# A first conditioning computed by halves, its second half behind the first projections of an attention layer

## The reference

```python
def _bi_wkv(r, k, v, w, u, time_emb):          # r = x, k = v = f
    tf = sigmoid(sum(time_emb, axis=-1))
    decay = exp(-exp(w)) * (0.5 + 0.5 * tf)
    ek = exp(minimum(k, 30.0)); ekv = ek * v
    # nf, df: a = a * decay + ekv_t, b = b * decay + ek_t, forward in time; nb, db backward
    euk = exp(minimum(u + k, 30.0))
    num = nf + nb - ekv + euk * v
    den = df + db - ek + euk
    return sigmoid(r) * (num / maximum(den, 1e-08)) * (0.8 + 0.2 * tf)
x = x + attention(_bi_wkv(x, f, f, L0_cond_w, L0_cond_u, cond))     # 32 query heads, 8 key heads, rope, causal softmax
x = x + ffn(_bi_wkv(x, f, f, L0_cond2_w, L0_cond2_u, cond))         # and so on, three more layers
```

## Time and profile before

| | us |
|---|---|
| median of 3 runs (lowest, highest) | 1380.36 (1378.04, 1382.36) |
| the profiled execution | 1380.08 |
| its span in the trace | 1378.3 |
| start and pieces of conditioning 0, until VectorE's last quotient | 0 to 62.3 |
| first matmul | 65.31 |
| first row maxima (group 0) | 82.90 |
| normalization of groups 0, 16, 32, 48, 63 starts at | 89.76, 159.67, 235.68, 311.67, 380.23 |
| end of the attention stage, next stage's sigmoid | 393.20 |

### The profile page before, as it was taken

One profiled execution on the slowest core, in us unless ns is written; L12 is line 12 of the kernel. 1 busy time (PEld: TensorE's weight loads), 2 busy tenths in 40 slices (PEclk: granted clock), 3 DMA queues, 4 the chain that ended last, 5 costly groups with the idle time before them and its releaser, 6 DMA issues. The chain is left out here.

```text
span 1378.3 us, 16687 instructions
## 1 busy us (share of the span) xinstructions
PE 1143.8 (83%) x5770; PEld 824.8 (60%) x5770; DVE 976.2 (71%) x1977; ACT 611.9 (44%) x1423; POOL 535.9 (39%) x440
## 2 busy tenths in 40 slices
PE   0179899999979888999599957999999966189997
PEld 0045556555557765333388846888888842068876
DVE  7868988888758996944533536888888868954354
ACT  2156666666655545345154424333333326033333
POOL 4437767676503221530064323444444410405520
PEclk9999999999989999999699978999999988579999
DMA  2032122121011102200543421111010000011101
GB/s 93 12 88 56 38 50 62 39 63 26 21 33 46 39 24 82 102 0 1 204 153 135 174 73 56 32 32 32 32 31 31 5 8 31 0 48 46 46 28 61
DMA packets 31091, 73.41 MB, mean 53 GB/s; under 512 B 5362, under 2 KB 15091, under 8 KB 28192
## 3 DMA queue, kind: packets, MB, share of 16 engines
q1 hardware_dynamic: 28432, 67.44, 15.8%
q0 software_dynamic: 1536, 3.86, 0.9%
q10 hardware_dynamic: 1040, 1.05, 0.2%
HBM read 55.89 MB, written 6.29 MB: 45 GB/s over the span
## 5 line engine op out<-in xcount | busy, mean ns | idle before, releaser
L175 POOL TENSOR_TENSOR sums<-scans 128x512 f32<-128x512 f32 x64 | 88.2, 1378 | 314.1 <-ACT terms L169 173.0
L531 ACT ACTIVATE probs<-ps_s,stats 128x256 f32<-128x256 f32 (+1 forms) x256 | 104.3, 419 | 58.9 <-DVE stats L621 57.5
L722 PE MATMUL ps_p<-xin,wkvq 128*128 128x512 f32 x148 | 74.0, 624 | 67.6 <-DVE xin L238 65.3
L195 DVE RECIPROCAL sums<-sums 128x256 f32<-128x256 f32 x64 | 112.1, 1752 | 2.0
L478 POOL TENSOR_TENSOR probs<-probs,stats 128x512 f32<-128x512 f32 x64 | 67.4, 1053 | 118.6 <-DVE stats L627 118.6
L621 DVE CUSTOM_DVE_ANT_0 ps_s<-ps_s,mask 128x256 f32<-128x256 f32 (+1 forms) x256 | 82.9, 383 | 8.9 <-PE ps_s L746 8.7
L180 POOL TENSOR_TENSOR sums<-sums,terms 128x512 f32<-128x512 f32 x64 | 85.5, 1336 | 5.0
L722 PEld LDWEIGHTS ps_p<-xin,wkvq 128*128 128x128 f32 x148 | 26.5, 199 | 88.5 <-issue 84.8
L920 POOL TENSOR_TENSOR L3hid<-L3hid,L3sig 128x1024 f32<-128x1024 f32 x17 | 46.1, 2719 | 75.4 <-DVE L3hid L1046 37.8
L1888 PE MATMUL K_ps_kvp<-K_wqkv_hi,K_xin_hi 128*128 128x256 f32 x256 | 75.4, 294 | 0.0
L1793 ACT ACTIVATE K_ks<-K_ps_kvp 128x256 f32<-128x256 f32 x64 | 24.6, 385 | 110.9 <-PE K_ps_kvp L1888 110.9
(11 more groups left out here) (393 smaller groups left out, 3449.9 us busy)
## 6 DMA issues: line engine op xcount, KB each, us to landing
E_fc<-l_fc_dram SPq DMA_DIRECT2D x16, 1024.0 KB, 7.2
qswap<-qraw SPq DMA_DIRECT2D x60, 128.0 KB, 2.3
K_wqkv<-l_wqkv_dram SPq DMA_DIRECT2D x16, 384.0 KB, 3.2
L3wgu<-L_w_dram SPq DMA_DIRECT2D x17, 256.0 KB, 2.6
L0wgu<-L_w_dram SPq DMA_DIRECT2D x14, 256.0 KB, 2.6
L3wdn<-L_w_dram SPq DMA_DIRECT2D x17, 128.0 KB, 2.1
wkvq<-w_l0a_dram SPq DMA_DIRECT2D x4, 512.0 KB, 4.2
wo<-w_l0a_dram SPq DMA_DIRECT2D x4, 512.0 KB, 3.7
```

Of the source, the lines that this page charges most:

```text
L175: pstep.mark(pool.tensor_tensor(sums[:, k, :, :], scans[:, k, :, 0, :], scans[:, k, :, 1, :], ALU.add))
L195: dstep.mark(dve.reciprocal(den, den))
L531: ins = act.activation(dst[:, i % 2, :], src[:, i % 2, :], ACT.Exp, bias=stats[:, g % 4, 4 + i:5 + i], scale=-1.0, accum_out=stats[:, g % ...
L722: ins = pe.matmul(ps[:, :], w[:, k, :], xin[:, k, h * HALF:(h + 1) * HALF], start=(k == 0), stop=(k == CH - 1))
```

## The change

Conditioning 0 is computed in the order `HALF_FIRST`, so that the first four pieces give the first half of the columns. Five pieces (with four quotients) and the product of the first half stay in `stage_first`; the barrier comes then, and the three other pieces, the last four quotients and the second half's product follow inside the attention stage. `START` projects the first half first: k0, q00, v0, q10. Its last two items run behind the scores of groups 0 and 1. The pieces of conditioning 1 go 1, 2, 2, 3 over the pairs. In `stage_first` the loads are reordered (`crep`, `vecs`, then `fside` by halves), and bound, exponential and inner product also go by halves, the second inner product behind the scans of the second piece. Shifts of the rotation in pair 0: the second half's `rope_first` in group 1 rather than 0, `rope_cos`, `rope_sin`, `rope_add` of q1 one group later.

```diff
+HALF_FIRST = (0, 1, 4, 5, 2, 3, 6, 7)
...
-                sp.dma_start(fside[:, :, :], io["fT"]).then_inc(s_f, 16)
+                sp.dma_start(crep[:, :, :], io["cond"]).then_inc(s_c, 16)
                 sp.dma_start(vecs[:, :], io["vecs"]).then_inc(s_vec, 16)
-                sp.dma_start(crep[:, :, :], io["cond"]).then_inc(s_c, 16)
+                for h in range(2):
+                    sp.dma_start(fside[:, :, halves[h]], io["fT"][:, :, halves[h]]).then_inc(s_f[h], 16)
...
+                for p in range(FIRST_PIECES):
+                    if p == FIRST_PIECES - 1:
+                        act.wait_ge(s_x, 16)
+                        condition_act(act, sig_first)
+                    piece_act(act, 0, HALF_FIRST[p], p % 2)
...
-                block_dve(dve, 0)
+                for p in range(FIRST_PIECES):
+                    if p == FIRST_PIECES - 1:
+                        dve.wait_ge(s_ekv, 2)
+                    piece_scans(dve, 0, HALF_FIRST[p], p % 2)
+                    if p == 1:
+                        bound_inner(1)
+                    if p:
+                        piece_finish(dve, 0, HALF_FIRST[p - 1], (p - 1) % 2)
+                dstep.wait()
+                condition_half(dve, 0, sig_first, 0)
...
-            START = ("k0", "q00", "k1", "q01", "v0", "v1", "q10", "q11")
+            START = ("k0", "q00", "v0", "q10", "k1", "q01", "v1", "q11")
+            AHEAD = 6
...
-                condition_act(act, sig)
-                for what in START:
-                    evac(0, what)
+                for p in range(FIRST_PIECES, NP):
+                    piece_act(act, l, HALF_FIRST[p], p % 2)
+                    for what in START[2 * (p - FIRST_PIECES):2 * (p - FIRST_PIECES) + 2]:
+                        evac(0, what)
...
+                        if g < len(START) - AHEAD:
+                            evac(0, START[AHEAD + g])
...
-                condition_dve(dve, l, sig)
+                for p in range(FIRST_PIECES, NP):
+                    piece_scans(dve, l, HALF_FIRST[p], p % 2)
+                    piece_finish(dve, l, HALF_FIRST[p - 1], (p - 1) % 2)
+                dve.wait_ge(s["ld_rope"], 32)
+                rope_first(0, "k", 0)
+                rope_first(0, 0, 0)
+                piece_finish(dve, l, HALF_FIRST[NP - 1], (NP - 1) % 2)
+                dstep.wait()
+                condition_half(dve, l, sig, 1)
+                for h, what, step in ((0, "k", 1), (0, "k", 2), (0, 0, 1), (0, 0, 2)):
+                    rope_first(h, what, step)
...
-                        if g == 0:
+                        if g == 1:
...
-                        if u in (0, 3):
+                        if u in (0, 3) and c:
                             for step in (0, 1, 2) if u == 0 else (3, 4):
-                                piece_scan(dve, l + 1, 2 * c, 0, step)
...
+                        if c == LAST and u in (12, 13):
+                            for step in (0, 1, 2) if u == 12 else (3, 4):
+                                piece_scan(dve, *next_piece(NP - 1), step)
                 pt_evac(ALL - 3)
                 recip(ALL - 1)
                 pt_evac(ALL - 2)
                 pt_evac(ALL - 1)
+                piece_finish(dve, *next_piece(NP - 1))
...
-                for what in START:
+                for what in START[:AHEAD]:
                     item(0, what)
                 for c in range(L0_PAIRS):
                     for u in range(NU):
                         g = c * NU + u
                         score(g)
+                        if g < len(START) - AHEAD:
+                            item(0, START[AHEAD + g])
```

More of the change, by code:

```diff
@@ L144, in turn_of @@
     def turn_of(l, i):
+        if l < 2:
+            return NP * l + HALF_FIRST.index(i)
         group = next(g for g in TOGETHER if l in g)
@@ L229, in condition_act, with condition_half @@
             act.activation(sig[:, :, half], xT[:, :, half], ACT.Sigmoid).then_inc(sig_ready, 1)
[L231 to L236, removed]
+    def condition_half(dve, l, sig, h):
+        dve.wait_ge(sig_ready, 2 * l + h + 1)
+        for b in (2 * h, 2 * h + 1):
             c = slice(b * T, (b + 1) * T)
@@ L262, in stage_first @@
             block = st.enter_context(nc.Block())
+            halves = (slice(0, HALF), slice(HALF, NT))
             @block.sync
             def _(sp):
-                sp.dma_start(fside[:, :, :], io["fT"]).then_inc(s_f, 16)
+                sp.dma_start(crep[:, :, :], io["cond"]).then_inc(s_c, 16)
                 sp.dma_start(vecs[:, :], io["vecs"]).then_inc(s_vec, 16)
-                sp.dma_start(crep[:, :, :], io["cond"]).then_inc(s_c, 16)
+                for h in range(2):
+                    sp.dma_start(fside[:, :, halves[h]], io["fT"][:, :, halves[h]]).then_inc(s_f[h], 16)
                 sp.dma_start(xT[:, :, :], io["xT"]).then_inc(s_x, 16)
@@ L308, in _ @@
                                             small[:, 2 * NB + b:2 * NB + b + 1], None, ALU.mult)
+                bound_inner(0)
                 dstep.link(ins)
@@ L397, in turned, with next_piece @@
                 return 5 * n + {0: 3, "k": 4, 1: 5, 2: 6, 3: 7}[what]
+            def next_piece(p):
+                return l + 1, HALF_FIRST[p], p % 2
             def swap_q(i):
@@ L642, in _ @@
                 dve.tensor_tensor(cols[:, 16:32], cols[:, 0:16], vecs[:, four:four + 16], ALU.mult).then_inc(s["cols_ready"], 1)
-                condition_dve(dve, l, sig)
+                for p in range(FIRST_PIECES, NP):
+                    piece_scans(dve, l, HALF_FIRST[p], p % 2)
[4 more added lines that the diff above has]
+                piece_finish(dve, l, HALF_FIRST[NP - 1], (NP - 1) % 2)
+                dstep.wait()
+                condition_half(dve, l, sig, 1)
+                for h, what, step in ((0, "k", 1), (0, "k", 2), (0, 0, 1), (0, 0, 2)):
+                    rope_first(h, what, step)
                 for ch in range(CH):
                     dstep.link(dve.tensor_scalar(xT[:, ch, :], xT[:, ch, :], vec("bo0", ch), None, ALU.add))
-                dve.wait_ge(s["ld_rope"], 32)
-                for h, what, step in ((0, "k", 0), (0, 0, 0), (0, "k", 1), (0, "k", 2), (0, 0, 1), (0, 0, 2),
-                                      (1, "k", 0), (1, 0, 0)):
-                    rope_first(h, what, step)
+                rope_first(1, "k", 0)
+                rope_first(1, 0, 0)
                 for c in range(L0_PAIRS):
@@ L664, in _ @@
                             wo_add(4 * c + LAST_PART[u] + 1, LAST_PART[u], ps_p[:, :])
-                        if u in (1, 5, 9):
+                        if u == (1 if c else 2):
+                            rope_sin(c, 1)
+                        if u == (2 if c else 3):
+                            rope_add(c, 1)
+                        if u in (5, 9):
                             rope_sin(c, 1 + u // 4)
-                        if u in (2, 6, 10):
+                        if u in (6, 10):
                             rope_add(c, 1 + u // 4)
```

90 lines of the change are left out of this document (55 added, 35 removed).

## The result

The changed kernel takes 1372.29 us (median of 8 runs, 1370.03 to 1375.79), the one before 1379.63 (8 runs): ratio 0.9943 with a 95% interval of 0.9934 to 0.9953. By the ratio that is 7.9 us less (6.5 to 9.1); the two medians lie 7.3 us apart. Forecast were 11 us less, with 1363.5 to 1375.5 as the range. The profiled execution has a span of 1370.8 us, 7.5 less.

A forecast was written before the change was run, and what follows sets the result against it. VectorE was taken to bound the time to the first projection and pair 0, with room in pair 3. Terms -10.0 - 2.0 + 0.7 = -11.3 us took 1380.08 to 1368.8 profiled, median 1369; range 1363.5 to 1375.5 (8 in 10).

The forecast's parts named there:

- The start, -2.9 us: Up to the first `uk`: reordered loads and halved operations bring it to 9.1 instead of 12.09 us; bounds -1.5 to -3.5.
- Inner product, first product, barrier, rotation: VectorE work added among the first eight pieces: 1.15 + 2.13 + 1.38 us, so the last quotient ends at 64.0.
- k1 and q01, 6.1 us: TensorE's first items after its idle time run at 1.2 GHz, from 65.5 to 71.6 us.
- Group 4, -10.0: Row maxima of group 4 in pair 0 come at 90.4 instead of 100.43 us; bounds -7 and -12.6.
- Rest of pair 0, -2.0: Behind group 4, groups 7 and 8 lose a quotient of 2.4 us; 2.0 taken as gain, bounds 0 to 3.5.
- Pair 3, +0.7: Added scans and quotient in pair 3 mostly hidden in VectorE's idle time; cost 0.7 us, +5.0 with no cover.
- (d): Slower: TensorE falls to 1.2 GHz and stays there through pair 0; 1397 us, chance 0.04.
- (a): Less gain: rotation, swap and `rope_cos` chain sets pair 0; about -5.5, 1375 us; chance 0.22 together with (c).
- (b): More gain: k1 starts at 2.4 GHz (-2.6) and waits for GpSimd vanish (-1.5); 1364.5 us, chance 0.10.
- (c): Pair 3's third piece is paid in full, +5.0 instead of +0.7; 1373 us; chance 0.22 together with (a).

The follow-up runs named there:

- keeping the clock: The changed kernel with 15 more matmuls that nobody reads on TensorE between q10 and k1: 1368.81 us, ratio 0.9923 to the kernel before.

## Why the prediction was right, and where its sizes were off

- **The mechanism** held at each place: TensorE's first four items go beside the pieces, k1 begins when k0 did (66.30 and 65.31; forecast 65.5), group 0 is 8.7 us earlier (forecast 9.5), pairs 1 and 2 are unchanged, pair 3 pays little. That the work beside the pieces carries half of the gain is shown by taking it away (+4.1 us).
- **The start, -2.9 us: too large.** It was -1.8 here and between -1.9 and +0.7 in the other traces with it. I put the second half of `fside` at 6.3 us; it landed at 7.5 to 10.0. The step that failed is the estimate of the loads, and I had not seen that the bound of the second half stands ahead of work that needs the first alone.
- **Inner product, first product, barrier, rotation: +4.66 forecast.** From the first `uk` to the end of the last quotient it was 50.19 us before and 54.43 now, +4.2.
- **k1 and q01, 6.1 us: right within its spread** (6.4 here, 5.1 to 6.6 over the traces), and worth about 3 us, shown by keeping the clock.
- **Group 4, -10.0: -7.9.** Of the missing 2.1 us 0.8 are k1's later start (66.30 for 65.5: 1.1 too much at the start, 0.4 too little in the next term), 0.3 k1 and q01. The rotation of the second half took 3.85 us (77.83 to 81.68) instead of 2.8, because GpSimd's normalization lies beside it; I had applied the hold to one place and not to this. It reaches group 4 by a path that the sum doesn't have: group 2's maxima, group 1's normalization, `rope_cos` (86.07 to 89.41), `rope_add`.
- **Rest of pair 0, -2.0: -1.0.** 59.24 us from group 4's maxima to group 16's normalization before, 58.23 now. With two pieces in pair 0 it was 59.9, so the lighter pair is worth 1.7 there. The rest is the clock, a term that the sum puts at nothing: in the nine traces in which it did not fall behind group 4, the same stretch takes 56.8 us, 2.4 less than before and near the forecast. What decides in which execution the clock falls there, no run shows.
- **Pair 3, +0.7: +0.36.** The last quotient was hidden as forecast.
- **The rivals.** (d) happened in part, without turning the sign: the clock fell around the gaps (0.54 from 54 to 66, 0.79 from 82 to 90, 0.57 from 92 to 96) and came back each time. What it costs: 3.5 us by the medians for the second start; 4.4 by the traces in the changed kernel's own order (318.26 to an estimated 313.8 with k1 and q01 at 2.4 GHz too); 5.9 and 6.5 with q11 and `rope_cos` ahead, which alone gave next to nothing. (a) is right in that swap and `rope_cos` form a chain of their own to group 4 (rotating earlier gave nothing), but it comes once, and the 2.0 of the rest of pair 0 are not lost to it. (b) adds up to 1364.7 by its own terms, not 1364.5. (c) is not what happened.

## What to carry to other kernels

Work that is moved beside another engine's list leaves a gap where it came from; on TensorE that gap was paid again here by a slow start, and a few matmuls that nobody reads, in the gap, won it back. Before a load is cut in halves, look at what stands in order behind the wait for the second half. When a wait is removed and the time stays, read the same place again: here the swap, `rope_cos` and the clock each stood ready to set group 4. And before two single traces are compared, look at the granted clock in each stretch between the two marks: here one fall more or less was worth 1.4 us, as much as some of the edits.

## What the hardware showed that I had not expected

- After 13.6 to 15.1 us without work TensorE's rise to 2.4 GHz came 3.1 to 6.1 us after k1's start, after three and a half to seven of the eight 128x512 float32 records of k1 and q01, by the same instructions.
- TensorE fell to 1.2 GHz again behind waits of 1.9 to 3.4 us. After the 3.36 us before 81.74 group 2's scores took 1.25 us instead of 0.92; after the 1.95 us before 91.55 the clock was at 0.57 from 92 to 96, while with the rotation in group 0 a wait of 2.05 us at the same place was followed by no fall. The same place behind group 4 showed a fall in four traces and none in nine, in the changed kernel both times; each fall took 1.4 us, and pair 0 never gave them back.
- Two loads of 512 KB, one after the other and behind two small ones, landed at 6.2 and 7.5 us in one execution and at 5.9 and 10.0 in another; one load of 1024 KB issued first landed at 5.7 in both traces that have it.
